# A graph-network kernel on one core: h0 remade by ScalarE and beta added by VectorE after the loop, the last chunk's pieces two maps later

## The chip, the cores and the metric

One core of a Trainium2 chip runs the whole kernel. The metric is the device time of one execution in microseconds; the trace is that of one profiled execution, and its times are microseconds from the start of its span. TensorE is PE in the rows (its weight loads PEld), VectorE is DVE, ScalarE is ACT, GpSimd is POOL, and SyncE, which issues most transfers, is SP. L893 is line 893 of the kernel.

## What is computed

Two graph layers over N = 1250 nodes with D = 512 features and E = 40000 edges (src, dst, and an edge tensor of 40000 x 512). Cut to what matters here:

```
h0  = relu(layernorm(x))
agg = segment_sum((h0[src] + edge) @ Wm.T + bm, dst) / max(deg, 1)
u   = concat(h0, agg) @ Wu.T + bu
o   = h0 + gelu(u)
x1  = x + layernorm(o) * gamma + beta
h1  = relu(layernorm(x1))
out = x1 + h1 + relu(((1 + eps) * h1 + segment_sum(h1[src], dst)) @ W1 + b1) @ W2 + b2
```

## The kernel before

Nodes lie in NT = 10 blocks of 128 rows. The kernel builds a matrix A16 of edge counts (node by node), so that a segment sum of gathered rows is a product with it. Node features that are multiplied with the counts are kept as a high and a low part, Hh and Hl, whose sum is the feature; Hl shares its memory with X.

**Stage 1, the edge loop** (to about 273 us). TensorE sums the edge tensor by destination and counts edges, VectorE and GpSimd add the results into aggT and A16, and in its last part the products "counts by h0" start, called pieces. A piece is one block of h0 against one chunk of columns: `PIECES` lists chunk 0 (512 columns), chunk 1 (512) and chunk 2 (256), ten pieces each. Also in this loop ScalarE makes h0 from x with scale rs and bias nb of the first layer norm (L478).

**Stage 2, the rounds after the loop** (about 276 to 351 us), where the change is. Each engine has its own queue, written out by hand, and each waits on semaphores. For each block b:

- TensorE: map b (`map_agg`, L1183: aggT times CT, four 128x512 fp32 products), which waits until VectorE has done update b-2. Between the first maps stand the ten pieces of chunk 2 (`late`, in the counts 1, 2, 3, 3, 1 behind maps 0 to 4). From map 5 on, map b is followed by T b-5 (`transpose_h1`), and from map 6 on by A b-6 (`times_A`: counts by h1, 512 columns, banks 0, 1, 4 and 5). After map 9 and A 3 come T 5, A 4, B 0, T 6, A 5, B 1, T 7, A 6, B 2, B 3, T 8 and so on (B is `times_A` with 256 columns), and behind them chunks C and E.
- VectorE works in rounds k = 0 to 14. The list STEPS (L919) says which step of which block stands in a round: update k (L866), center k-2 (L887), add_h0 k-1 (L871), add_x k-2 (L893), o_moments k-1 (L875), shift k-3 (L909), x1_moments k-2 (L897), four short steps, low_h1 k-4 (L914). Ahead of round 4 VectorE waits for all pieces and adds the sums of chunk 2 to aggT (L924, shown as L862), and TensorE waits for that sum after map 5, before T 0.
- ScalarE in step k: full_conv k+2 (L544, counts to fp32), gelu k (L548), h1 k-3 (L554), h1_high k-3 (L558), h1T k-3 (L563), which waits for T k-3.
- GpSimd: two small powers for each block (L424 rs, L428 rs2), and, for each block, `ahead(b)`: xt += beta (L413), and h0t = Hh + Hl (L416). Blocks 0 to 2 are done before the rounds; from block 3 on, `ahead(b)` falls into VectorE's round b.
- SP: loads the tile xt of x for block b once add_x b-3 has freed one of the three buffers (L339).

So add_h0 b needs gelu b and h0t b; add_x b needs rs b and xt b with beta in it; h1 b is written over Hh b, so it waits until h0t b has been made and until chunk 2's piece b has been read.

**Stage 3** (from about 351 us): TensorE finishes the products with the counts, then the two dense layers W1 and W2.

Of the kernel before, what the change touches and what calls it, by code (L numbers as in the profile page):

```python
# [5 lines left out]
F32 = mybir.dt.float32  # L6
# [4 lines left out]
ALU = mybir.AluOpType  # L11
ACT = mybir.ActivationFunctionType
AX = mybir.AxisListType

P = 128
# [12 lines left out]
def gnn_kernel(nc, x, src, dst, edge, Wm, bm, Wu, bu, gamma, beta, W1, b1, W2, b2, eps, out):  # L28
# [3 lines left out]
    NT = -(-N // P)  # L32
# [47 lines left out]
    def place(name, shape, dt, offset=None):  # L80
        size = mybir.dt.size(dt)
        for n in shape[1:]:
            size *= n
        if offset is None:
            offset = at[0]
            at[0] += -(-size // 32) * 32
        return nc.alloc_sbuf_tensor_at(name, shape, dt, offset=offset), offset

    X, x_at = place("X", [P, NT, D], F32)
    Hl, _ = place("Hl", [P, NT, D], F32R, x_at)  # L90
    Hh, _ = place("Hh", [P, NT, D], F32R)
    U, u_at = place("U", [P, NT, D], F32)
# [3 lines left out]
    CT, _ = place("CT", [P, FC, D], F32)  # L96
    W1s, _ = place("W1s", [P, FC, HID], F32, w1_at)
    W2s, _ = place("W2s", [P, KC, D], F32, a16_at)
    WuN, _ = place("WuN", [P, FC, 2 * D], F32, agg_at)
    Wu2T, _ = place("Wu2T", [P, FC, D], F32, u_at + 10240)  # L100
    WmN, _ = place("WmN", [P, FC, D], F32, u_at)
    bmB, _ = place("bmB", [P, FC, P], F32, u_at + 8192)
    acc, _ = place("acc", [P, NP], U16, w1_at)
    Dsum, _ = place("Dsum", [P, NP], F32, w1_at + NP * 2)
    TB = 3
    xt = [place(f"xt{i}", [P, D], F32, w1_at + i * 2048)[0] for i in range(TB)]
# [10 lines left out]
    ARd, _ = place("ARd", [P, NT, 256], F32R, arc_at + NT * 256 * 4)  # L117
    AR, _ = place("AR", [P, NT, NP], F32R, stream_at)
    hid, _ = place("hid", [P, KC, NP], F32, stream_at)
# [4 lines left out]
    dst_i, _ = place("dst_i", [P, GE], I32, arc_at + 8 * GE * 4)  # L124
    src_i, _ = place("src_i", [P, GE], I32, arc_at + 9 * GE * 4)
    genE, _ = place("genE", [P, SUB, D], F32, arc_at)
    genD, _ = place("genD", [P, SUB, P], F32, arc_at + SUB * D * 4)
    genS, _ = place("genS", [P, SUB, P], BF16, arc_at + SUB * D * 4 + SUB * P * 4)
    genK, _ = place("genK", [P, SUB, P], BF16, arc_at + SUB * D * 4 + SUB * P * 6)
# [5 lines left out]
    rest, _ = place("rest", [P, D], F32, idx_at)  # L135
    assert TB * 2048 <= 5 * SUB * GP * 4
    h0t = [place(f"h0t{i}", [P, D], F32)[0] for i in range(TB)]
    iotaF, _ = place("iotaF", [P, P], F32)
    iotaP, _ = place("iotaP", [P, 256, 2], BF16)
# [21 lines left out]
    nunc, _ = place("nunc", [1, 2], I32)  # L161
    stats, _ = place("stats", [P, NT, 6], F32)
    mv, _ = place("mv", [P, NT, 2], F32)
    stats2, _ = place("stats2", [P, NT, 6], F32)
    mv2, _ = place("mv2", [P, NT, 2], F32)
    ve, _ = place("ve", [P, NT], F32)
    ve2, _ = place("ve2", [P, NT], F32)
    rs, _ = place("rs", [P, NT], F32)
    rs2, _ = place("rs2", [P, NT], F32)
    nb, _ = place("nb", [P, NT], F32)  # L170
    degs, _ = place("degs", [P, NT], F32)
    rdeg, _ = place("rdeg", [P, NT], F32)
# [4 lines left out]
    with ctx:  # L177
# [61 lines left out]
        o_sum = sem("o_sum")  # L239
# [117 lines left out]
        def _(pool):  # L357
# [20 lines left out]
            nc.gpsimd.tensor_scalar(big[G, :], big[G, :], 1.0, None, ALU.subtract).then_inc(outside_ready, 1)  # L378
            pool.wait_ge(consts, 4)
            pool.wait_ge(ve_ready, 1)  # L380
            nc.gpsimd.tensor_tensor(rs[:], ve[:], mhalf[:], ALU.pow).then_inc(rs_ready, 1)

            def low_h0(b):
                pool.wait_ge(hi0_ready, b + 1)
# [23 lines left out]
                        low_h0(b)  # L408
            pool.wait_ge(low0_ready, NT)

            def ahead(b):
                pool.wait_ge(xt_in[b % TB], 16 * (b // TB + 1))
                nc.gpsimd.tensor_tensor(xt[b % TB][:], xt[b % TB][:], betaB[:], ALU.add).then_inc(xb_ready, 1)  # L413
                if b >= TB:
                    pool.wait_ge(o_sum, b - TB + 1)
                nc.gpsimd.tensor_tensor(h0t[b % TB][:], Hh[:, b, :].bitcast(F32), Hl[:, b, :].bitcast(F32), ALU.add).then_inc(h0t_ready, 1)  # L416

            pool.wait_ge(late_in, 48)
            for b in range(TB):
                ahead(b)  # L420
            for k in range(NT + 1):
                if k < NT:
                    pool.wait_ge(ve1_ready, k + 1)
                    nc.gpsimd.tensor_tensor(rs[:, k:k + 1], ve[:, k:k + 1], mhalf[:, 0:1], ALU.pow).then_inc(rs1_ready, 1)  # L424
                if k > 0:
                    b = k - 1
                    pool.wait_ge(ve2_ready, b + 1)
                    nc.gpsimd.tensor_tensor(rs2[:, b:b + 1], ve2[:, b:b + 1], mhalf[:, 0:1], ALU.pow).then_inc(rs2_ready, 1)  # L428
                    if b + TB < NT:
                        ahead(b + TB)  # L430

            pool.wait_ge(h1_ready, NT)
            pool.wait_ge(split1, NT)
# [10 lines left out]
        def _(act):  # L444
# [30 lines left out]
            def h0(b):  # L475
                if b == 0:
                    act.wait_ge(nb_ready, 1)
                nc.scalar.activation(X[:, b, :], X[:, b, :], ACT.Relu, bias=nb[:, b:b + 1], scale=rs[:, b:b + 1]).then_inc(h0_ready, 1)  # L478

            def transposed_h0(b):  # L480
                act.wait_ge(hT_mm, b + 1)
# [61 lines left out]
            def full_conv(c):  # L543
                nc.scalar.copy(AR[:, c, :], A16[:, c, 0:NP]).then_inc(conv, 1)  # L544

            def gelu(b):
                act.wait_ge(t_ready, b + 1)
                nc.scalar.activation(tt[b % TB][:], tt[b % TB][:], ACT.Gelu).then_inc(g_ready, 1)  # L548

            def h1(b):  # L550
                act.wait_ge(nb2_ready, b + 1)
                act.wait_ge(h0t_ready, b + 1)
                act.wait_ge(piece_mm, 2 * NT + b + 1)
                nc.scalar.activation(X[:, b, :], U[:, b, :], ACT.Relu, bias=nb[:, b:b + 1], scale=rs2[:, b:b + 1]).then_inc(h1_ready, 1)  # L554

# [9 lines left out]

            act.wait_ge(eps_ready, 2)
            full_conv(0)
            full_conv(1)
            for k in range(NT + 4):
                if k + 2 < NT:  # L570
                    full_conv(k + 2)
                for work, lag in ((gelu, 0), (h1, 3), (h1_high, 3), (h1T, 3)):
                    if 0 <= k - lag < NT:
                        work(k - lag)

            act.wait_ge(rst_mm, 4)

# [12 lines left out]
        def _(dve):  # L590
# [153 lines left out]
            for n in range(NG):  # L744
# [23 lines left out]

                if n == 2:
                    dve.wait_ge(rs_ready, 1)  # L770
                    V.scalar_tensor_tensor(nb[:], mv[:, :, 0], -1.0, rs[:], ALU.mult, ALU.mult).then_inc(nb_ready, 1)
                if n - 1 in ASIDE:
                    kind, k = ASIDE[n - 1]
                    if kind == "product" and k == FC:
# [110 lines left out]
            def center(b):  # L885
                dve.wait_ge(o_aggr, b + 1)
                V.scalar_tensor_tensor(tt[b % TB][:], tt[b % TB][:], mv[:, b, 0:1], gammaB[:], ALU.subtract, ALU.mult).then_inc(centered, 1)  # L887

            def add_x(b):
                dve.wait_ge(centered, b + 1)  # L890
                dve.wait_ge(rs1_ready, b + 1)
                dve.wait_ge(xb_ready, b + 1)
                V.scalar_tensor_tensor(U[:, b, :], tt[b % TB][:], rs[:, b:b + 1], xt[b % TB][:], ALU.mult, ALU.add).then_inc(x1_ready, 1)  # L893

            def x1_moments(b):
                dve.wait_ge(x1_ready, b + 1)
                V.bn_stats(stats2[:, b, :], U[:, b, :]).then_inc(x1_stats, 1)  # L897

            def x1_moments2(b):
                dve.wait_ge(x1_stats, b + 1)  # L900
                V.bn_aggr(mv2[:, b, :], stats2[:, b, :]).then_inc(x1_aggr, 1)

            def x1_variance(b):
                dve.wait_ge(x1_aggr, b + 1)
# [6 lines left out]
            def low_h1(b):  # L911
# [4 lines left out]
            dve.wait_ge(late_in, 48)  # L916
            dve.wait_ge(deg_step, 3 + NT)

            STEPS = [(update, 0), (center, 2), (add_h0, 1), (add_x, 2), (o_moments, 1), (shift, 3), (x1_moments, 2), (o_moments2, 1),  # L919
                     (x1_moments2, 2), (o_variance, 1), (x1_variance, 2), (low_h1, 4)]  # L920
            for k in range(NT + 5):
                if k == 4:
                    dve.wait_ge(piece_mm, 3 * NT)
                    add_sums(packed(0), QS[2][0]).then_inc(agg_done, 1)  # L924
                for work, lag in STEPS:
                    if 0 <= k - lag < NT:
                        work(k - lag)
# [23 lines left out]
        def _(pe):  # L951
# [223 lines left out]
            def transpose_h1(b):  # L1175
                pe.wait_ge(h1_ready, b + 1)
                if b >= 2:
                    pe.wait_ge(h1T_done, b - 1)
                for f in range(FC):
                    last = T.transpose(ps[:, 6 + b % 2, f * P:(f + 1) * P], X[:, b, f * P:(f + 1) * P], ident[:])  # L1180
                last.then_inc(h1T_mm, 1)
# [17 lines left out]
            def late(count):  # L1199
                for _ in range(count):  # L1200
                    piece(late_pieces.pop(0))

            for b in range(5):
                map_agg(b)
                late((1, 2, 3, 3, 1)[b])
            assert not late_pieces
            for b in range(5, NT):
                map_agg(b)
                if b == 5:
                    pe.wait_ge(agg_done, 2 * FC + 1)  # L1210
                transpose_h1(b - 5)
                if b > 5:
                    times_A(b - 6, "A")
            pe.wait_ge(t_ready, NT)
# [73 lines left out]
```

## Time and profile before

| | us |
|---|---|
| median of 3 runs | 529.69 (528.18 to 530.55) |
| profiled execution, its own time | 526.39 |
| its span in the trace | 524.6 |
| TensorE busy in the span | 482.8 (92%) |
| VectorE busy | 283.0 (54%) |
| GpSimd busy | 166.8 (32%) |
| ScalarE busy | 147.5 (28%) |
| mean granted TensorE clock, as a share | 0.992 |

The profiled execution took 1.8 us more than its span, and 3.3 us less than the median of the runs. Busy shares are averages over three stages with different limits, so the rows below are read for the rounds after the loop alone.

### The profile page before, as it was taken

How to read it: one execution, taken by the hardware profiler on the slowest of the kernel's cores; microseconds unless marked ns; L12 is line 12 of the kernel's file. 1: busy time of each engine (PE TensorE's matmuls, PEld its weight loads, DVE VectorE, ACT ScalarE, POOL GpSimd, SP SyncE). 2: the span in 40 equal slices, each digit the busy share in tenths (PEclk: the TensorE clock that was granted, in tenths of full speed). 3: DMA queues.
4: the chain of work that ended last, by engine and by line, in shares of the span. 5: the costliest groups of instructions: out<-in, count | busy, mean ns of one | idle time of the engine just before them, and what ended most of it. 6: DMA issues, size and time to landing. Idle time of an engine off the chain costs nothing.

```text
span 524.6 us, 8826 instructions
## 1 busy us (share of the span) xinstructions
PE 482.8 (92%) x3003; PEld 277.0 (53%) x3003; DVE 283.0 (54%) x660; ACT 147.5 (28%) x291; POOL 166.8 (32%) x217
## 2 busy tenths in 40 slices
PE   5889999898898988999999999599989999999997
PEld 4446554444444544675665655379944446744442
DVE  6897887888777779645434789983000000011111
ACT  4416644123222223222237245441011122100000
POOL 7323665333322224000023267636994000000000
PEclk9999999999999999999999999799999999999999
DMA  8998998889999999988820111112040000011111
GB/s 299 316 367 301 338 327 292 348 342 361 352 367 358 374 363 390 408 308 315 271 82 2 32 29 41 35 62 100 1 163 0 0 0 1 0 41 40 41 40 35
DMA packets 31115, 98.95 MB, mean 189 GB/s; under 512 B 3577, under 2 KB 3577, under 8 KB 31067
## 3 DMA queue, kind: packets, MB, share of 16 engines
q1 hardware_dynamic: 30458, 97.27, 50.7%
q10 hardware_dynamic: 608, 1.05, 0.7%
q8 instruction: 28, 0.46, 0.4%
q14 instruction: 21, 0.16, 0.1%
HBM read 95.76 MB, written 2.56 MB: 187 GB/s over the span
## 4 chain that ended last, share of the span: by engine, by line
PE 63%; DVE 21%; issue 6%; PEld 6%; DVEq 1%; POOL 1%; DMA 1%; SPq 0%; PEldq 0%; POOLq 0%
PE ps L1260 13%; PE ps L1245 13%; PE ps L1007 9%; PE ps L1048 7%; DVE A L669 5%; PE ps L1105 5%; PE ps L1106 4%; PE ps L1018 4%; PE ps L1194 3%; PEld ps L1171 3%; PE ps L1036 3%; PEld ps L1172 2%; DVE U L893 2%; DVE tt L871 2%; DVE oneS L648 2%
## 5 line engine op out<-in xcount | busy, mean ns | idle before, releaser
L400 POOL TENSOR_TENSOR aggT<-turned_sums,aggT 128x88 f32 x118 | 53.9, 456 | 107.4 <-ACT turned_sums L473 94.4
L1007 PE MATMUL ps<-ea,oneD 128*22 128x256 f32 x1264 | 83.9, 383 | 1.4 <-DVE oneD L640 0.9
L947 DVE TENSOR_TENSOR U<-ps,U 128x512 f32<-128x512 f32 (+1 forms) x10 | 6.9, 692 | 130.8 <-PE ps L1260 130.8
L467 ACT COPY packed_sums<-ps 128x256 f32<-128x256 f32 x79 | 29.4, 372 | 163.9 <-PE ps L1007 163.9
L1245 PE MATMUL ps<-aggT,W1s 128*128 (+1 forms) x192 | 67.4, 513 | 2.2 <-PEq L1239 2.2
L1260 PE MATMUL ps<-W2s,hid 128*128 128x512 f32 (+1 forms) x160 | 68.8, 592 | 0.0
L669 DVE TENSOR_TENSOR A<-ps,A 128x220 f32 x158 | 60.3, 381 | 8.6 <-PE ps L1018 8.0
L1018 PE MATMUL ps<-oneK,oneS 128*128 128x220 bf16 x316 | 42.5, 259 | 14.7 <-DVE oneS L648 13.0
L1245 PEld LDWEIGHTS ps<-aggT,W1s 128*128 128x128 f32 x192 | 36.4, 190 | 33.1 <-issue 33.0
L1007 PEld LDWEIGHTS ps<-ea,oneD 128*22 128x22 f32 x1264 | 30.5, 101 | 41.1 <-issue 23.6
L648 DVE TENSOR_TENSOR oneK<-iotaP,P_key 128x880 bf16<-128x880 bf16 x79 | 51.8, 655 | 0.0
L1260 PEld LDWEIGHTS ps<-W2s,hid 128*128 128x128 f32 (+1 forms) x160 | 30.0, 188 | 38.2 <-issue 38.2
L1171 PE MATMUL ps<-AR,Hh 128*128 128x256 f32 (+1 forms) x160 | 45.2, 318 | 0.5
L1172 PE MATMUL ps<-AR,Hl 128*128 128x256 f32 (+1 forms) x160 | 44.0, 312 | 0.0
L640 DVE TENSOR_TENSOR oneD<-iotaF,T_srel 128x88 f32<-128x88 f32 x79 | 22.4, 283 | 37.0 <-PE ps L1007 35.8
L1018 PEld LDWEIGHTS ps<-oneK,oneS 128*128 128x128 bf16 x316 | 28.9, 97 | 21.2 <-DVE oneK L648 11.7
L648 DVE TENSOR_TENSOR oneS<-iotaP,P_lo 128x512 bf16<-128x512 bf16 x79 | 39.2, 496 | 0.0
L1194 PE MATMUL ps<-CT,aggT 128*128 128x512 f32 x80 | 36.0, 593 | 1.2 <-DVE aggT L720 1.2
L581 ACT ACTIVATE hid<-ps,b1C 128x512 f32 (+1 forms) x24 | 14.6, 608 | 80.3 <-PE ps L1245 80.3
L1048 PE MATMUL ps<-Wu1T,U 128*128 128x512 f32 x80 | 36.1, 593 | 0.0
L1036 PE MATMUL ps<-ident,packed_sums 128*128 128x128 f32 x158 | 34.5, 300 | 0.0
L1105 PE MATMUL ps<-ARc,Hh 128*128 128x512 f32 x80 | 33.4, 417 | 1.0 <-DVE aggT L720 1.0
(139 smaller groups left out, 645.1 us busy)
## 6 DMA issues: line engine op xcount, KB each, us to landing
ea<-in_edge_attr_dram SPq DMA_DIRECT2D x78, 1024.0 KB, 7.6
X<-in_x_dram SPq DMA_DIRECT2D x1, 2304.0 KB
xt<-in_x_dram SPq DMA_DIRECT2D x9, 256.0 KB, 2.7
out_dram<-U SPq DMA_DIRECT2D x9, 256.0 KB
W1s<-in_L_gnn_W_dram SPq DMA_DIRECT2D x1, 2048.0 KB, 7.7
W2s<-in_L_gnn_W_dram SPq DMA_DIRECT2D x1, 2048.0 KB, 8.7
WuN<-in_L_gnn_Wu_dram ACTq DMA_DIRECT2D x1, 1024.0 KB, 5.4
WuN<-in_L_gnn_Wu_dram SPq DMA_DIRECT2D x1, 1024.0 KB, 6.8
```

Source lines behind the costliest of these rows:

```text
L400: nc.gpsimd.tensor_tensor(cols, sums, cols, ALU.add).then_inc(early_step, 1)
L648: V.tensor_tensor(hot[m % HOTS][:], iota, mine, ALU.is_equal).then_inc(ready, 1)
L669: V.tensor_tensor(cols, ps[:, 4 + m % 2, half * KW:(half + 1) * KW].rearrange("p (h w) -> p h w", w=W), cols, ALU.add).then_inc(add_step, 1)
L1007: last = T.matmul(to.rearrange("p (c d) -> p c d", c=2), oneD[h][:, g * 2 + j, :], data, start=j == 0, stop=j == 1)
L1018: last = T.matmul(ps[:, 4 + m % 2, (j // 2) * KW:(j // 2 + 1) * KW], oneS[h][:, j // 2, :, j % 2], oneK[h][:, j // 2, :, j % 2], start=j % ...
L1048: last = T.matmul(ps[:, ASIDE_BANK["u1", b], :], U[:, b, f * P:(f + 1) * P], Wu1T[:, f, :], start=f == 0, stop=f == FC - 1)
L1105: T.matmul(to, Hh[:, c, rows], counted, start=c == 0 and (q < 2 or f % 2 == 0), stop=False)
L1171: T.matmul(to, Hh[:, b, rows], AR[:, b, start:start + cols], start=b == 0 and (cols == 512 or f % 2 == 0), stop=False)
L1172: last = T.matmul(to, Hl[:, b, rows], AR[:, b, start:start + cols], start=False, stop=b == NT - 1 and (cols == 512 or f % 2 == 1))
L1194: last = T.matmul(ps[:, 2 + b % 2, :], aggT[:, f, b * P:(b + 1) * P], CT[:, f, :], start=f == 0, stop=f == FC - 1)
L1245: last = T.matmul(ps[:, CHUNK_BANK[k % 4], 0:cols], W1s[:, f, k * P:(k + 1) * P], aggT[:, f, bass.ds(start, cols)], start=f == 0, stop=f = ...
L1260: last = T.matmul(ps[0:rows, 6 + b % 2, :], hid[:, k, b * P:b * P + rows], W2s[:, k, :], start=k == 0, stop=k == KC - 1)
```

## The change

The first layer norm's scale and bias get tiles of their own, rs0 and nb0, so that they outlive the loop (rs and nb are written again for the second and third norm). After the loop ScalarE makes h0t b from the loaded tile xt b with `relu(rs0 * x + nb0)`, one step ahead of its use, between gelu and h1. VectorE adds beta to xt b in a new step `add_beta` (lag 1) between x1_moments and o_moments2, once h0t b is made. GpSimd's `ahead` is gone, so GpSimd only makes the powers. The pieces of chunk 2 stand in the counts 0, 0, 2, 3, 3 and 2 behind maps 0 to 5; VectorE adds their sums ahead of round 6 instead of round 4, and TensorE waits for that after map 6 and T 1, before A 0. The moments of x1 share the tile stats with those of o.

```diff
@@ gpsimd
-            nc.gpsimd.tensor_tensor(rs[:], ve[:], mhalf[:], ALU.pow).then_inc(rs_ready, 1)
+            nc.gpsimd.tensor_tensor(rs0[:], ve[:], mhalf[:], ALU.pow).then_inc(rs_ready, 1)
...
-            def ahead(b):
-                pool.wait_ge(xt_in[b % TB], 16 * (b // TB + 1))
-                nc.gpsimd.tensor_tensor(xt[b % TB][:], xt[b % TB][:], betaB[:], ALU.add).then_inc(xb_ready, 1)
-                if b >= TB:
-                    pool.wait_ge(o_sum, b - TB + 1)
-                nc.gpsimd.tensor_tensor(h0t[b % TB][:], Hh[:, b, :].bitcast(F32), Hl[:, b, :].bitcast(F32), ALU.add).then_inc(h0t_ready, 1)
-
-            pool.wait_ge(late_in, 48)
-            for b in range(TB):
-                ahead(b)
...
-                    if b + TB < NT:
-                        ahead(b + TB)
@@ scalar
-                nc.scalar.activation(X[:, b, :], X[:, b, :], ACT.Relu, bias=nb[:, b:b + 1], scale=rs[:, b:b + 1]).then_inc(h0_ready, 1)
+                nc.scalar.activation(X[:, b, :], X[:, b, :], ACT.Relu, bias=nb0[:, b:b + 1], scale=rs0[:, b:b + 1]).then_inc(h0_ready, 1)
...
+            def h0_again(b):
+                act.wait_ge(xt_in[b % TB], 16 * (b // TB + 1))
+                if b >= TB:
+                    act.wait_ge(o_sum, b - TB + 1)
+                nc.scalar.activation(h0t[b % TB][:], xt[b % TB][:], ACT.Relu, bias=nb0[:, b:b + 1], scale=rs0[:, b:b + 1]).then_inc(h0t_ready, 1)
...
             def h1(b):
                 act.wait_ge(nb2_ready, b + 1)
-                act.wait_ge(h0t_ready, b + 1)
...
             full_conv(0)
+            h0_again(0)
             full_conv(1)
...
                         work(k - lag)
+                    if work is gelu and k + 1 < NT:
+                        h0_again(k + 1)
@@ vector
-                    V.scalar_tensor_tensor(nb[:], mv[:, :, 0], -1.0, rs[:], ALU.mult, ALU.mult).then_inc(nb_ready, 1)
+                    V.scalar_tensor_tensor(nb0[:], mv[:, :, 0], -1.0, rs0[:], ALU.mult, ALU.mult).then_inc(nb_ready, 1)
...
+            def add_beta(b):
+                dve.wait_ge(h0t_ready, b + 1)
+                V.tensor_tensor(xt[b % TB][:], xt[b % TB][:], betaB[:], ALU.add).then_inc(xb_ready, 1)
...
-                V.bn_stats(stats2[:, b, :], U[:, b, :]).then_inc(x1_stats, 1)
+                V.bn_stats(stats[:, b, :], U[:, b, :]).then_inc(x1_stats, 1)
...
-            STEPS = [(update, 0), (center, 2), (add_h0, 1), (add_x, 2), (o_moments, 1), (shift, 3), (x1_moments, 2), (o_moments2, 1),
+            STEPS = [(update, 0), (center, 2), (add_h0, 1), (add_x, 2), (o_moments, 1), (shift, 3), (x1_moments, 2), (add_beta, 1), (o_moments2, 1),
                      (x1_moments2, 2), (o_variance, 1), (x1_variance, 2), (low_h1, 4)]
             for k in range(NT + 5):
-                if k == 4:
+                if k == 6:
                     dve.wait_ge(piece_mm, 3 * NT)
                     add_sums(packed(0), QS[2][0]).then_inc(agg_done, 1)
@@ tensor
             for b in range(5):
                 map_agg(b)
-                late((1, 2, 3, 3, 1)[b])
-            assert not late_pieces
+                late((0, 0, 2, 3, 3)[b])
             for b in range(5, NT):
                 map_agg(b)
                 if b == 5:
+                    late(2)
+                    assert not late_pieces
+                transpose_h1(b - 5)
+                if b == 6:
                     pe.wait_ge(agg_done, 2 * FC + 1)
-                transpose_h1(b - 5)
                 if b > 5:
                     times_A(b - 6, "A")
```

## Rows read from the trace of the kernel before

**Rows 1.** Busy time of each engine in two stretches, granted clock, DMA.

```profile
309.50:351.30 41.80, 34.06 (x132) 22.15 (x132) 41.70 (x79) 22.14 (x32) 27.00 (x24) 0.92 0.08 25
351.30:385.00 33.70, 31.59 (x253) 30.30 (x252) 8.12 (x10) 3.16 (x5) 25.31 (x21) 1.00 0.16 63
```

**Rows 2.** Timeline of DVE, round 6: start, us, line, operation.

```profile
316.51 0.74 DVE L866 SCALAR_TENSOR_TENSOR tt<-ps,rdeg,U 128x512 f32<-128x512 f32 x1
317.17 0.74 DVE L887 SCALAR_TENSOR_TENSOR tt<-tt,mv,gammaB 128x512 f32<-128x512 f32 x1
317.83 1.79 DVE L871 TENSOR_TENSOR tt<-tt,h0t 128x512 f32<-128x512 f32 x1
319.54 1.75 DVE L893 SCALAR_TENSOR_TENSOR U<-tt,rs,xt 128x512 f32<-128x512 f32 x1
```

**Rows 3.** Timeline of POOL in the same round.

```profile
316.97 0.54 POOL L428 TENSOR_TENSOR rs<-ve,mhalf 128x1 f32<-128x1 f32 x1
317.49 1.58 POOL L413 TENSOR_TENSOR xt<-xt,betaB 128x512 f32<-128x512 f32 x1
319.03 1.71 POOL L416 TENSOR_TENSOR h0t<-Hh,Hl 128x512 f32<-128x512 f32 x1
```

**Rows 4.** Timeline of DVE, round 10.

```profile
344.43 0.74 DVE L887 SCALAR_TENSOR_TENSOR tt<-tt,mv,gammaB 128x512 f32<-128x512 f32 x1
345.09 0.68 DVE L871 TENSOR_TENSOR tt<-tt,h0t 128x512 f32<-128x512 f32 x1
345.69 0.75 DVE L893 SCALAR_TENSOR_TENSOR U<-tt,rs,xt 128x512 f32<-128x512 f32 x1
```

**Rows 5.** Timeline of PE: T 5, T 6, T 7, first product of A 6.

```profile
338.25 1.12 PE L1180 MATMUL ps<-ident,X 128*128 128x128 f32 x4 [5.49 <-DVE tt L866]
...
343.79 0.66 PE L1180 MATMUL ps<-ident,X 128*128 128x128 f32 x4
...
348.01 0.66 PE L1180 MATMUL ps<-ident,X 128*128 128x128 f32 x4 [0.38 <-ACT X L554]
348.79 0.50 PE L1171 MATMUL ps<-AR,Hh 128*128 128x512 f32 x1
```

**Rows 6.** Stretches of 2 us, columns as in rows 1: PE's clock.

```profile
335.00:337.00 2.00, 0.00 (x0) 0.00 (x0) 2.00 (x9) 1.03 (x2) 0.14 (x1) 0.68 0.23 75
...
341.00:343.00 2.00, 2.00 (x9) 1.62 (x8) 2.00 (x4) 0.08 (x1) 0.67 (x1) 0.61 0.00 0
...
383.00:385.00 2.00, 0.00 (x0) 0.00 (x0) 1.15 (x1) 0.00 (x0) 1.84 (x3) 1.00 0.00 0
```

**Rows 7.** Timeline of DVE: chunk 2's sum and the start of round 5.

```profile
303.51 1.23 DVE L862 TENSOR_TENSOR aggT<-ps,aggT 128x1024 f32<-128x1024 f32 x1 [1.97 <-PE ps L1106]
...
309.52 0.74 DVE L866 SCALAR_TENSOR_TENSOR tt<-ps,rdeg,U 128x512 f32<-128x512 f32 x1
```

**Rows 8.** Timeline of PE: T 0, T 1, map 7, T 2.

```profile
306.74 0.60 PE L1180 MATMUL ps<-ident,X 128*128 128x128 f32 x4
...
310.61 0.60 PE L1180 MATMUL ps<-ident,X 128*128 128x128 f32 x4
...
312.92 3.59 PE L1194 MATMUL ps<-CT,aggT 128*128 128x512 f32 x8
316.35 0.60 PE L1180 MATMUL ps<-ident,X 128*128 128x128 f32 x4
```

**Rows 9.** L478 by source: ns min/median/max, first and last start.

```profile
L478 ACT ACTIVATE X<-X,nb,rs x10: 814/824/830, 43.6 to 68.1; 128x512 f32<-128x512 f32 x10
```

**Rows 10.** Timeline of ACT in round 6.

```profile
316.99 0.69 ACT L563 ACTIVATE aggT<-ps,eps 128x512 f32<-128x512 f32 x1 [0.52 <-PE ps L1180]
317.58 1.25 ACT L544 CAST AR<-A 128x1280 fp32r<-128x1280 uint16 x1
318.73 0.63 ACT L548 ACTIVATE tt<-tt 128x512 f32<-128x512 f32 x1
```

**Rows 11.** The ten loads of xt, from issue to landing.

```profile
DMA to landing us min/median/max: 2.6/2.7/5.1
```

More of the change, by code:

```diff
@@ L163, in gnn_kernel @@
     mv, _ = place("mv", [P, NT, 2], F32)
-    stats2, _ = place("stats2", [P, NT, 6], F32)
     mv2, _ = place("mv2", [P, NT, 2], F32)
@@ L169, in gnn_kernel @@
     rs2, _ = place("rs2", [P, NT], F32)
+    rs0, _ = place("rs0", [P, NT], F32)
+    nb0, _ = place("nb0", [P, NT], F32)
     nb, _ = place("nb", [P, NT], F32)
@@ L896, in x1_moments @@
                 dve.wait_ge(x1_ready, b + 1)
-                V.bn_stats(stats2[:, b, :], U[:, b, :]).then_inc(x1_stats, 1)
+                V.bn_stats(stats[:, b, :], U[:, b, :]).then_inc(x1_stats, 1)
             def x1_moments2(b):
                 dve.wait_ge(x1_stats, b + 1)
-                V.bn_aggr(mv2[:, b, :], stats2[:, b, :]).then_inc(x1_aggr, 1)
+                V.bn_aggr(mv2[:, b, :], stats[:, b, :]).then_inc(x1_aggr, 1)
             def x1_variance(b):
```

## The prediction, made before the changed kernel was run

> **What bounds the kernel now.** I read the share of each engine in the stretch of the rounds first. From 309.5 to 351.3 us VectorE is busy for 41.70 of 41.80 us and TensorE for 34.06; from 351.3 to 385 it is the other way round, TensorE 31.59 of 33.70 and VectorE 8.12 [rows 1]. So VectorE sets the pace up to about 349 us, TensorE behind it, and what is saved in VectorE's rounds counts until TensorE is the bound.
>
> Then I read one round on VectorE beside GpSimd's queue. Round 6 begins at 316.51; the five rounds 5 to 9 begin at 309.52 [rows 7] and are over at 344.43 [rows 4], 6.98 us each. In it add_h0 takes 1.79 us and add_x 1.75 [rows 2], while in round 10 the same two take 0.68 and 0.75 [rows 4]. The difference between them is GpSimd: in round 6 its add of beta runs from 317.49 to 319.07 and its Hh + Hl from 319.03 to 320.74 [rows 3]; add_h0 begins at 317.83 and lets add_x begin at 319.54, half a microsecond (its own length) after the first of them ended, and add_x in turn is as long as it takes to outlast the second. In round 10 GpSimd has no such work. So VectorE stands still while GpSimd's add runs. The records differ by 1.79 - 0.68 = 1.1 and 1.75 - 0.75 = 1.0: 2.1 us in each of five rounds are spent waiting for GpSimd, and a clean round is 6.98 - 2.10 = 4.88. (A record is some 0.08 longer than the step to the next start, 0.68 against 0.60; from here on I count steps: add_h0 0.60, add_x 0.67, update and center 0.66.)
>
> Last I read TensorE. It waits 5.49 us ahead of T 5 for update 9, and a slower clock follows: T 5 takes 1.12 us where T 6 takes 0.66 [rows 5]; the granted clock is 0.68 at 335 to 337 and 0.61 at 341 to 343 (1.00 is 2.4 GHz, 0.50 is 1.2), and full at 383 to 385, where TensorE was idle too [rows 6]. A 6 starts at 348.79 [rows 5], and from there TensorE runs without a gap. **A 6's start is the point that I forecast; what it gains, the end gains.**
>
> **The change, part by part.**
>
> *Names of loop tiles, stats.* rs0, nb0 and the shared stats move no work: the same instructions in the same order. Nothing, from both sides.
>
> *GpSimd's twenty adds go.* Of these ten stand in rounds 5 to 9 and cost VectorE 5 x 2.1 = **-10.5 us**. The other ten stand ahead of the rounds and in rounds 3 and 4, where VectorE waits for the pieces in the end (1.97 us idle ahead of the sum [rows 7]); they save nothing.
>
> *VectorE's add_beta.* It has the form of add_h0, 0.60 us from start to next start [rows 4]. Before A 6 six rounds carry it (5 to 10): 6 x 0.60 = **+3.6 us**. It could collide with GpSimd's powers. Row first: the power at 316.97 runs to 317.51 beside center, issued at 317.17, and center takes its usual 0.74 [rows 2, 3]. The Trainium skill's page "SBUF — State Buffer", section "Who interferes with whom", says that a VectorE instruction with two SBUF inputs and a GpSimd one that reads SBUF lock each other out for the whole instruction. By that, center would have waited 0.34 us, and the sum would carry up to 5 x 0.34 = 1.7 us more; the row says zero for a 128x1 power, and the trace agrees with the page only for the large adds. I take zero, and keep 1.7 for the range.
>
> *ScalarE's h0.* An activation of this form took 824 ns [rows 9]. ScalarE is busy for 22 of 41.8 us [rows 1], so seven more (blocks 3 to 9 in the rounds) fit in total; the question is who stands behind. Behind h0 b+1 in its queue stand h1 b-3, h1_high, h1T, full_conv and gelu b+1, and T b-3 and add_h0 b+1 wait for these. h0 b also waits for its tile, freed by add_x b-3 in VectorE's round b-1, 2.6 us into it (update 0.66, center 0.66, add_h0 0.60, add_x 0.67), and landed after 0.3 us of issue and 2.7 us (5.1 at most) [rows 11]. From there h0, h1, h1_high, h1T, full_conv and gelu need 0.83 + 0.83 + 0.65 + 0.59 + 1.15 + 0.55 = 4.6 us (h1 taken like h0, h1_high like a gelu with its wait) [rows 9, 10], and add_h0 b wants gelu b 1.3 us into round b+1. Rounds of 5.5: 5.5 - 2.6 + 5.5 + 1.3 = 9.7, less 4.6 leaves 5.1 us for the landing. It is hidden at 2.7 and just hidden at 5.1.
>
> *The pieces and the sum of chunk 2.* A piece costs TensorE the same wherever it stands; T 0 comes after six maps and all ten pieces in both, so it stays at 306.74 [rows 8]. VectorE's rounds 0 to 4 have slack up to there. The sum (303.51 to the next start at 304.65, 1.14 us) [rows 7] moves from ahead of round 4, where VectorE was waiting anyway, to ahead of round 6, where it is on the path: **+1.1 us**. And TensorE, which did not wait for it before, now has only A 0 left to do after T 1 and waits until VectorE has finished round 5 and the sum.
>
> *The walk.* I go through the queues with these durations: map 3.43, T and A together 2.31, T alone 0.4 (0.78 where TensorE had stopped, as at T 7), A 1.9, B half of that; 0.64 from T's start until ScalarE's h1T starts [rows 5, 8, 10].
>
> 1. T 0 at 306.7 releases low_h1 0 (0.61), the last step of round 4; update 5 at 308.0, against 309.52 [rows 7]: **-1.5 us**.
> 2. ScalarE: h1T 0 from 307.4, full_conv, gelu 4 done 309.7; add_h0 4 would like 309.3, waits 0.4. From there a round needs 4.16 (4.88 + 0.60 - 1.32). Round 5 ends 313.9, the sum 315.05.
> 3. T 1 waits for h1 1 behind h0 5: 311.4. TensorE then idles about 2.9 us until the sum at 315.05. A 0, map 7, T 2 at 320.4. Low_h1 2 waits for T 2, 1.2 us; update 7 at 321.7.
> 4. T 2, h1T 2, full_conv, gelu 6 (0.64 + 0.59 + 1.15 + 0.55): add_h0 6 at 323.4, 0.4 late; update 8 at 327.6. In the same way, 0.3 late, update 9 at 333.4.
> 5. T 5 waits for h1 5 behind h0 9 on ScalarE: 335.4, against 338.25, and at full clock. T 6 339.1. Round 9 ends 338.9, round 10 (no update) takes 4.82: low_h1 6 done 343.7, **A 6 at 343.8**.
>
> As a sum, up to the end of round 10: -10.5 + 3.6 + 1.1 - 1.5 + waits of 0.4 + 1.2 + 0.4 + 0.3 = 2.3, together **-5.0 us**. A 6 at 343.8 against 348.79 is the same 5.0. Behind it, T 8, T 9 and their h1 come as early, and stage 3 stands on TensorE alone. Span 524.6 - 5.0 = 519.6, own time 526.4 - 5.0 = 521.4. The profiled execution is 3.3 us under the median of the runs, so the median to expect is 529.69 - 5.0 = **524.7**. Half a per cent, about what a measurement can tell from no change here, is 2.65 us.
>
> The gain has a ceiling. Without any wait or slow clock in this stretch TensorE would save its idle 41.80 - 34.06 = 7.7 us [rows 1], and for the slow clock 1.9 (5.54 from T 5 to T 6, where T, A and B with the restart need 3.6 [rows 5]): 9.6 us.
>
> **Rivals.**
>
> *The clock falls at the new gap.* TensorE idles some 2.9 us ahead of A 0. In the trace it idled from 338.25 - 5.49 = 332.8 [rows 5], and the clock was down between 335 and 337 [rows 6], so a gap of about 3 us can be enough; the shorter one up to 385 was not. Price: the half clock cost 1.9 us from T 5 to T 6; A 0 and map 7 stand on the path that sets update 7 and all after it, so about 1.8 comes through. A 6 at 345.6, gain 3.2: **526.5**. The Trainium skill's page "TensorE: Matmul & The Clock Gate", Part 1, has throttling as the default state, which comes back when the array goes idle; it speaks against putting a wait where none was.
>
> *More is gained.* If gelu and h1 come earlier than I have them (rounds 7 to 10 without the 0.7 of waits, and TensorE's gap shorter because T 1 starts early), 7 us: **522.7**.
>
> *Within half a per cent.* Powers that lock (1.7) together with the slow clock (1.8) leave 1.5: **528.2**.
>
> *Slower: the load of the tile becomes the ring.* ScalarE's queue now stops at h0 for the tile, where GpSimd's did before and nobody stood behind. Up to 5.1 us of landing it is hidden; each microsecond more is then paid by one load after the other. Walking the queues with a landing of 8 us puts A 6 at 349, no gain; with 9 us at 352.2, 3.4 us later than before: **533.1**. For it: a wait in front of five others' work. Against: the loads took 2.6 to 5.1 [rows 11], with DMA nearly idle (0.08) [rows 1].
>
> *The change doesn't do it.* If the 1.1 us were not GpSimd's doing, VectorE would keep 6.98 and add 0.6: slower by 3. Against it stand the clean rows of round 10 [rows 4]; part of the slower chance.
>
> **How the numbers follow.** Forecast 0.48, clock 0.20, more 0.13, within half a per cent 0.11, slower 0.08. Forecast, more and most of the clock case are faster by over 2.65 us: 0.76. The same side takes 0.11 and the worse end of the clock case, 0.16; slower 0.08. The range reaches from 8 us gained (a step past the "more" case, within the ceiling of 9.6) to 0.9 gained (clock and powers together): 521.7 to 528.8. The likeliest case alone: 523.2 to 526.
>
> **What the new trace would show.** Right: add_h0 and add_x at 0.7 in all rounds; rounds of 5.5 to 6; sum of chunk 2 at about 314 and a gap of about 3 us on TensorE ahead of A 0; T 5 near 335.4 at full clock; A 6 near 343.8. Wrong: any 1.7 us step on VectorE; h0 waiting for the tile with VectorE waiting for gelu behind it; a granted clock under 1 between 312 and 320; T 0 later than 306.7, which would mean that the earlier rounds had no slack for ScalarE's new work.

## The result, and the profile after

| | before | changed |
|---|---|---|
| median of 10 runs, us | 528.18 (526.88 to 530.55) | 524.40 (521.50 to 526.09) |
| profiled execution, own time | 526.39 | 523.95 |
| its span | 524.6 | 522.2 |
| GpSimd busy in the span | 166.8 | 136.7 |

The ratio is 0.993, with a 95% interval from 0.991 to 0.995: 3.8 us faster, where 5.0 was forecast for the likeliest case and 3.2 for the case in which the clock falls. The time lies in the stated range of 521.7 to 528.8. That it lies within 0.3 us of the forecast median of 524.7 is luck: that median was counted down from 529.69, the median of three runs, and the ten runs of the kernel before have 528.18, from which 5.0 would have given 523.2.

The two stretches of [rows 1], in the changed kernel:

```profile
309.50:351.30 41.80, 36.19 (x153) 24.24 (x152) 36.59 (x87) 26.97 (x39) 9.94 (x13) 0.96 0.13 38
351.30:385.00 33.70, 31.66 (x241) 29.27 (x240) 7.08 (x7) 2.38 (x4) 26.50 (x21) 1.00 0.16 54
```

VectorE, which had no gap before (41.70 of 41.80 us busy), now has 5 us of them. Its timeline from the sum of chunk 2 to the start of round 7 answers to [rows 2] and [rows 7] (start, us, line, operation, idle time before and who ended it):

```profile
315.06 1.22 DVE L859 TENSOR_TENSOR aggT<-ps,aggT 128x1024 f32<-128x1024 f32 x1
316.19 0.74 DVE L863 SCALAR_TENSOR_TENSOR tt<-ps,rdeg,U 128x512 f32<-128x512 f32 x1
...
317.51 0.69 DVE L868 TENSOR_TENSOR tt<-tt,h0t 128x512 f32<-128x512 f32 x1
318.12 0.74 DVE L894 SCALAR_TENSOR_TENSOR U<-tt,rs,xt 128x512 f32<-128x512 f32 x1
...
320.04 0.68 DVE L888 TENSOR_TENSOR xt<-xt,betaB 128x512 f32<-128x512 f32 x1
320.63 0.18 DVE L876 BATCH_NORM_AGGREGATE mv<-stats 128x2 f32<-128x6 f32 x1
...
324.05 0.69 DVE L915 TENSOR_TENSOR Hl<-X,Hh 128x512 fp32r<-128x512 f32 x1 [2.99 <-PE ps L1181]
324.66 0.75 DVE L863 SCALAR_TENSOR_TENSOR tt<-ps,rdeg,U 128x512 f32<-128x512 f32 x1
326.38 0.69 DVE L868 TENSOR_TENSOR tt<-tt,h0t 128x512 f32<-128x512 f32 x1 [0.31 <-ACT tt L543]
```

add_h0 (L868) and add_x (L894) take 0.69 and 0.74 where they took 1.79 and 1.75. The new add of beta (L888) costs 0.59 to the next start. But low_h1 2 (L915) stands 2.99 us for T 2. The reason is in TensorE's timeline (T 0, A 0, T 2, T 5, T 7, A 6), which answers to [rows 5] and [rows 8]:

```profile
307.94 0.60 PE L1181 MATMUL ps<-ident,X 128*128 128x128 f32 x4
...
316.33 0.50 PE L1172 MATMUL ps<-AR,Hh 128*128 128x512 f32 x1 [3.28 <-DVE aggT L859]
...
323.35 0.60 PE L1181 MATMUL ps<-ident,X 128*128 128x128 f32 x4
...
338.17 0.63 PE L1181 MATMUL ps<-ident,X 128*128 128x128 f32 x4 [0.88 <-issue]
...
345.19 0.66 PE L1181 MATMUL ps<-ident,X 128*128 128x128 f32 x4 [0.37 <-ACT X L548]
346.50 0.50 PE L1172 MATMUL ps<-AR,Hh 128*128 128x512 f32 x1 [0.65 <-DVE Hl L915]
```

TensorE waits 3.28 us for the sum ahead of A 0, and then the clock is down (0.57 from 317 to 321, where 0.50 is 1.2 GHz). Stretches of 2 us (columns as in [rows 1]; the last is the gap ahead of the first dense layer, at full clock):

```profile
315.00:317.00 2.00, 0.67 (x3) 0.58 (x4) 2.00 (x4) 1.97 (x4) 1.07 (x2) 1.00 0.02 4
317.00:319.00 2.00, 2.00 (x7) 1.59 (x6) 2.00 (x4) 0.52 (x1) 0.00 (x0) 0.57 0.00 0
319.00:321.00 2.00, 2.00 (x4) 0.89 (x4) 2.00 (x8) 0.00 (x0) 0.00 (x0) 0.57 0.49 119
381.00:383.00 2.00, 0.36 (x1) 0.30 (x2) 0.86 (x1) 0.00 (x0) 1.84 (x3) 1.00 0.03 8
```

Since T 0 does not begin at the same moment in all traces (the time up to the first map, which the change leaves alone, was 1.2 us longer in this execution than in the one of before, and T 0 comes 30.1 us after the first map in every trace: 307.94 against 306.74), I measure from T 0 to A 6 from here on. Before it is 348.79 - 306.74 = **42.05 us**, now 346.50 - 307.94 = **38.56**: 3.5 us gained. The forecast was 37.1. Behind A 6 there is no difference: 175.8 us to the end of the span before, 175.7 now.

### The profile page after: what moved, and what is told of

It reads as the page before. It is cut to its first block, busy times and chain, and to the rows that moved or that the text cites. A ratio compares the mean times of both kernels' runs of the same rounds, so it can differ in the third digit from the quotient of the medians.

```text
span 522.2 us, 8832 instructions
## 1 busy us (share of the span) xinstructions
PE 482.2 (92%) x3003; PEld 276.5 (53%) x3003; DVE 277.4 (53%) x670; ACT 153.6 (29%) x301; POOL 136.7 (26%) x197
## 4 chain that ended last, share of the span: by engine, by line
PE 70%; DVE 14%; issue 6%; PEld 6%; DVEq 1%; DMA 1%; ACT 1%; POOL 0%; SPq 0%; PEldq 0%; ACTq 0%; POOLq 0%
PE ps L1263 13%; PE ps L1248 13%; PE ps L1008 10%; PE ps L1049 7%; PE ps L1195 5%; PE ps L1106 5%; DVE A L666 5%; PE ps L1107 4%; PE ps L1019 4%; PE ps L1037 3%; PEld ps L1172 3%; PE ps L975 3%; PEld ps L1173 2%; DVE oneS L645 1%; DVE oneD L637 1%
## 5 line engine op out<-in xcount | busy, mean ns | idle before, releaser
L415 POOL TENSOR_TENSOR rs<-ve,mhalf 128x1 f32<-128x1 f32 x10 | 7.8, 781 | 124.0 <-DVE ve L880 124.0
```

## The experiments

| kernel | median, us | ratio to before (95%) | T 0 to A 6, us | A 6 to the end, us |
|---|---|---|---|---|
| before | 528.18 | | 42.05 | 175.8 |
| changed, first | 524.40 | 0.993 (0.991 to 0.995) | 38.56 | 175.7 |
| changed, again | 523.93 | 0.993 (0.990 to 0.996) | 38.53 | 175.4 |
| engines only | 520.98 | 0.986 (0.982 to 0.989) | 35.23 | 177.3 |
| pieces only | 525.95 | 0.996 (0.994 to 0.998) | 40.75 | 177.3 |
| sum in round 4 | **518.78** | 0.983 (0.980 to 0.986) | 33.85 | 176.0 |
| GpSimd's adds as idle work | 532.08 | 1.009 (1.006 to 1.012) | 45.03 | 175.5 |
| memsets as idle work | 525.46 | 0.996 (0.993 to 0.998) | 38.50 | 178.3 |
| gap filled | 524.55 | 0.993 (0.990 to 0.996) | 36.97 | 178.2 |
| beta on GpSimd | 523.97 | 0.992 (0.989 to 0.995) | 38.44 | 175.7 |
| x tiles one load later | 528.10 | 1.000 (0.998 to 1.002) | 40.63 | 177.3 |
| x tiles two loads later | 528.56 | 1.002 (0.999 to 1.004) | 41.94 | 175.7 |

The last two columns come from one profiled execution of each kernel. The kernel before was run beside each group of kernels again (medians 528.15 to 528.68), and a ratio is to the runs beside it. The single runs of one kernel spread over some 4 to 5 us; the path from T 0 to A 6 is finer: the changed kernel gave 38.56 and 38.53.

**The changed kernel again**, as the mark for those below.

> The changed kernel itself, so that the others of this call are compared with it on the same chip. Both theories: about 3.8 us under the kernel before (0.993). In the trace, counted from T 0's start: TensorE waits about 3.3 us ahead of A 0, A 6 starts 38.6 us after T 0 where the clock falls in that gap and about 37 where it does not.

Both as before; the gap ahead of A 0 is 3.28 us again, and the clock falls in it again.

**Engines only.** The two halves of the change are parted: here the work moves from GpSimd to ScalarE and VectorE, and the pieces stay.

```diff
-                late((0, 0, 2, 3, 3)[b])
+                late((1, 2, 3, 3, 1)[b])
...
-                if k == 6:
+                if k == 4:
```

> ScalarE makes h0 and VectorE adds beta, but the pieces stand behind maps 0 to 4 as before, the sum of chunk 2 ahead of round 4, TensorE's wait for it ahead of T 0. Theory (all the gain is from GpSimd's adds that no longer stop VectorE, and moving the pieces costs some of it again through the gap ahead of A 0): no gap over 1.5 us on TensorE before T 5, full clock, A 6 some 35.8 us after T 0; 5.5 to 6.5 us under the kernel before, 1.5 to 3 under the changed one. Rival (the pieces had to move for the gain, since ScalarE's new work makes h1 0 late for the old order): 524 or more, no faster than the changed kernel, with TensorE waiting for h1.

Measured 7.2 us under before, somewhat more than expected, and 3.0 under the changed kernel. TensorE's longest wait between T 0 and A 6 is the one ahead of T 5, and the clock is full in all this stretch:

```profile
333.94 0.63 PE L1181 MATMUL ps<-ident,X 128*128 128x128 f32 x4 [1.82 <-DVE tt L863]
...
342.79 0.50 PE L1172 MATMUL ps<-AR,Hh 128*128 128x512 f32 x1 [0.65 <-DVE Hl L915]
```

T 1 does wait 0.8 us for h1 1, as the rival had it, but that is all. The whole gain is in this half, and the other half, the pieces and the sum of chunk 2 moved together, takes 3.3 us of it back on the path.

**Pieces only.** The other half alone, in the kernel before.

```diff
-                late((1, 2, 3, 3, 1)[b])
+                late((0, 0, 2, 3, 3)[b])
...
-                if k == 4:
+                if k == 6:
```

> The kernel before with only the pieces, the sum and TensorE's wait moved as in the change; GpSimd still adds beta and makes h0. Theory: VectorE's rounds 6 to 9 stay near 7 us, add_h0 and add_x at 1.7 us; round 5 begins some 1 us earlier, but the sum of 1.1 us and the gap ahead of A 0 are new: between 2 us faster and 2 us slower than before. Rival (the moved pieces bring the gain): 3 us or more faster than before.

2.2 us faster than before, 1.3 on the path: the same edit gains a little where GpSimd has its adds and costs 3.3 where it has not. Round 7, on VectorE and then on GpSimd:

```profile
324.06 0.84 DVE L914 TENSOR_TENSOR Hl<-X,Hh 128x512 fp32r<-128x512 f32 x1 [2.16 <-PE ps L1180]
324.83 0.74 DVE L866 SCALAR_TENSOR_TENSOR tt<-ps,rdeg,U 128x512 f32<-128x512 f32 x1
325.49 1.12 DVE L887 SCALAR_TENSOR_TENSOR tt<-tt,mv,gammaB 128x512 f32<-128x512 f32 x1
326.53 0.68 DVE L871 TENSOR_TENSOR tt<-tt,h0t 128x512 f32<-128x512 f32 x1
327.13 0.74 DVE L893 SCALAR_TENSOR_TENSOR U<-tt,rs,xt 128x512 f32<-128x512 f32 x1
```

```profile
323.08 1.28 POOL L413 TENSOR_TENSOR xt<-xt,betaB 128x512 f32<-128x512 f32 x1 [0.17 <-DMA xt<-in_x_dram]
324.32 1.74 POOL L416 TENSOR_TENSOR h0t<-Hh,Hl 128x512 f32<-128x512 f32 x1
```

The new wait of VectorE for T lies where GpSimd adds beta (from 323.08), so that this add stops VectorE for at most the 0.15 us by which low_h1 is longer; the second add stretches center, from 0.74 to 1.12, and add_h0 and add_x are back at 0.68 and 0.74 in this round. This does not hold for every round: in rounds 5 to 9 the stretched records of VectorE add up to some 6.3 us more than they take alone, against 10.5 in the kernel before. A wait and a lock that would each cost a microsecond or two cover each other in part. In the changed kernel there is no lock left to cover, and the wait is paid.

**Sum in round 4.** One step of the changed kernel moved: the sum of chunk 2 goes where VectorE stands anyway.

```diff
-                if k == 6:
-                    dve.wait_ge(piece_mm, 3 * NT)
-                    add_sums(packed(0), QS[2][0]).then_inc(agg_done, 1)
                 for work, lag in STEPS:
+                    if k == 4 and work is low_h1:
+                        dve.wait_ge(piece_mm, 3 * NT)
+                        add_sums(packed(0), QS[2][0]).then_inc(agg_done, 1)
```

> The changed kernel with one step moved: VectorE adds chunk 2's sum in round 4, right ahead of low_h1 0, where it stood still for 3.8 us waiting for T 0, instead of ahead of round 6. Theory (the gap ahead of A 0 and the fall of the clock in it are what the change gives back): the gap goes, the clock stays full, A 6 about 34.3 us after T 0, 4 us earlier than in the changed kernel's trace; 2.5 to 4.5 us under the changed kernel, 6.5 to 8.5 under the kernel before. Rival (the gap is hidden, since VectorE is the bound anyway): within 1 us of the changed kernel.

The fastest kernel of all: 5.2 us under the changed one and 9.4 under before, 0.7 and 0.9 more than the expected ranges reach; A 6 comes 33.85 us after T 0, 4.7 earlier than in the changed kernel. On VectorE, the sum fills what was idle time ahead of low_h1 0:

```profile
306.69 1.22 DVE L859 TENSOR_TENSOR aggT<-ps,aggT 128x1024 f32<-128x1024 f32 x1 [3.27 <-PE ps L1107]
307.83 0.68 DVE L915 TENSOR_TENSOR Hl<-X,Hh 128x512 fp32r<-128x512 f32 x1
```

The gap ahead of A 0 is gone and the clock is full at 309 to 315. This kernel has the pieces where the change put them, and A 6 comes 1.4 us earlier than with engines only (33.85 against 35.23). So it is not the moved pieces that cost the 3.3 us, but the place of the sum behind them.

**GpSimd's adds as idle work.** Does VectorE wait for what GpSimd computes, or for GpSimd being at work? The changed kernel, with two adds in each of the old places; their output is read by nobody.

```diff
+                    if b + TB < NT:
+                        for i in range(2):
+                            nc.gpsimd.tensor_tensor(idle[:], gammaB[:], betaB[:], ALU.add).then_inc(idle_step, 1)
+                            pool.wait_ge(idle_step, 2 * b + i + 1)
```

> The changed kernel, to which GpSimd's two 128x512 adds for each of the blocks 3 to 9 are given back as idle work: it adds two tiles that nobody changes into one that nobody reads, in the places where it added beta and made h0 before. Nothing waits for them. Theory (VectorE stands still while such an add runs): add_h0, add_x or their neighbours take about 1.1 us more in pairs again, rounds 5 to 9 grow by up to 2.1 us each, less where they waited for TensorE or ScalarE; A 6 comes 6 to 10 us later after T 0 than 38.5, and the kernel is 6 to 10 us slower than the changed one, slower than the kernel before. Rival (GpSimd's adds cost because VectorE had to wait for their results): no change, within 1 us of the changed kernel.

8.2 us slower than the changed kernel (532.08 against 523.93, on another chip; 1.009 and 0.993 of the kernel before, each beside its own runs), 6.5 on the path. Round 6, VectorE and then GpSimd:

```profile
317.78 1.01 DVE L890 SCALAR_TENSOR_TENSOR tt<-tt,mv,gammaB 128x512 f32<-128x512 f32 x1
318.71 1.76 DVE L874 TENSOR_TENSOR tt<-tt,h0t 128x512 f32<-128x512 f32 x1
320.39 0.74 DVE L900 SCALAR_TENSOR_TENSOR U<-tt,rs,xt 128x512 f32<-128x512 f32 x1
```

```profile
316.96 2.96 POOL L424 TENSOR_TENSOR idle<-gammaB,betaB 128x512 f32<-128x512 f32 x2
```

GpSimd's pair runs from 316.96 to 319.92, the first add until 318.24; center is stretched past the first and add_h0 past the second, and add_x behind them is not. Nobody used the result: it is the engine's work, not its data, that stops VectorE.

**Memsets as idle work.** The same with `nc.gpsimd.memset(idle[:], 0.0)` in place of the add.

> The same idle work as a 128x512 memset instead of an add, so GpSimd writes the tile but reads nothing. The Trainium skill, page SBUF - State Buffer, section Who interferes with whom, has VectorE's instructions with two SBUF inputs contend with a GpSimd instruction that reads SBUF, and not with one that only writes. By that, VectorE's records stay as in the changed kernel and the time is within 1 us of it. If any large GpSimd instruction stops VectorE, it is as slow as with the adds, in proportion to the length of the memsets.

On the path nothing: 38.50. The median is 1.5 us over the changed kernel's, more than the 1 us expected, though the two intervals overlap. The execution traced lost its time behind A 6 (178.3 against 175.7), where GpSimd makes no memset: TensorE waited 3.06 us ahead of the first dense layer instead of 2.04, and the clock fell there. Whether that explains the median is open. Two memsets (0.52 us each) beside center and add_h0, GpSimd and then VectorE:

```profile
331.47 1.10 POOL L424 MEMSET idle<- 128x512 f32 x2
```

```profile
331.17 0.74 DVE L890 SCALAR_TENSOR_TENSOR tt<-tt,mv,gammaB 128x512 f32<-128x512 f32 x1
332.16 0.69 DVE L874 TENSOR_TENSOR tt<-tt,h0t 128x512 f32<-128x512 f32 x1 [0.25 <-ACT tt L549]
```

Center runs into the first memset, and add_h0 is issued while the second runs; both take what they take alone. The Trainium skill's "SBUF — State Buffer", "Who interferes with whom", says that a VectorE instruction with two SBUF inputs meets only those of GpSimd's that read SBUF; by that rule, adds stop it and memsets don't, and both traces agree.

**Gap filled.** What does the clock's fall cost by itself? Idle products on TensorE in the gap, into a bank that T 2 overwrites.

```diff
                 if b == 6:
+                    pe.wait_ge(h1T_done, 1)
+                    for _ in range(3):
+                        T.matmul(ps[:, 6, :], ident[:], CT[:, 0, :], start=True, stop=True)
                     pe.wait_ge(agg_done, 2 * FC + 1)
```

> The changed kernel with three idle products of 512 columns (fp32, some 0.86 us each) on TensorE between T 1 and its wait for the sum of chunk 2, into a bank that the next transposes overwrite. The gap of 3.3 us shrinks to under 1. Theory (the clock's fall in the gap costs about 1.7 us, the gap itself stays): granted clock full from 312 to 321, A 6 about 36.9 us after T 0 instead of 38.5, and 1 to 2 us under the changed kernel. Rival (the slow clock is hidden behind VectorE, which is the bound): A 6 at 38.5 as before.

A 0 then waits only another 0.70 us, the clock stays full, and A 6 comes 36.97 us after T 0, 1.6 us earlier than in the changed kernel:

```profile
317.00:319.00 2.00, 2.00 (x9) 1.65 (x10) 2.00 (x4) 1.11 (x2) 0.00 (x0) 1.00 0.01 4
319.00:321.00 2.00, 2.00 (x6) 0.88 (x5) 2.00 (x5) 0.00 (x0) 0.00 (x0) 1.00 0.14 35
381.00:383.00 2.00, 0.39 (x1) 0.39 (x2) 0.00 (x0) 0.00 (x0) 1.69 (x2) 0.86 0.37 32
383.00:385.00 2.00, 2.00 (x3) 0.78 (x3) 0.00 (x0) 0.00 (x0) 1.99 (x2) 0.50 0.76 210
```

The median of 524.55 shows none of it. In the traced execution it was given back: the clock fell instead in the gap ahead of the first dense layer (the last two lines), and A 6 to the end took 178.2 us where the changed kernel took 175.7. Some 1.0 of these 2.5 us is not the clock but a longer wait ahead of the layer (3.00 us against 2.04), whose cause no run shows. Whether the medians agree for these reasons in all runs is open; only the path shows the 1.6.

**Beta on GpSimd.** ScalarE makes h0, GpSimd adds beta behind it, VectorE has no add_beta (the lines that call `ahead` are left out here).

```diff
-            STEPS = [(update, 0), (center, 2), (add_h0, 1), (add_x, 2), (o_moments, 1), (shift, 3), (x1_moments, 2), (add_beta, 1), (o_moments2, 1),
+            STEPS = [(update, 0), (center, 2), (add_h0, 1), (add_x, 2), (o_moments, 1), (shift, 3), (x1_moments, 2), (o_moments2, 1),
...
+            def ahead(b):
+                pool.wait_ge(h0t_ready, b + 1)
+                nc.gpsimd.tensor_tensor(xt[b % TB][:], xt[b % TB][:], betaB[:], ALU.add).then_inc(xb_ready, 1)
```

> The changed kernel with beta still added by GpSimd, once ScalarE has made h0; VectorE has no add_beta. Theory: one add for each round stops VectorE for about 1.1 us where VectorE saves 0.6: 5 x 0.5 = 2.5 us in rounds 5 to 9 less what the waits hide, so 0 to 3 us slower than the changed kernel. Rival (VectorE's extra 0.6 a round is the dearer of the two): 1 to 3 us faster.

No difference (38.44 against 38.5), but not for the reason given. In rounds 5 to 9 only two of the five adds stretch VectorE (center to 1.26 us in round 6, add_h0 to 1.77 in round 9); the other three are stretched themselves (1.74 us instead of 1.28). So VectorE paid some 1.6 us and was spared five times 0.6, and still nothing was gained: it waits 2.94 us for T 2 as before. Where the rest of the spared time went is not shown.

**X tiles landing later.** The slower rival: idle loads of the same size ahead of each x tile from block 3 on; the second kernel has 2 in both places where this diff has 1.

```diff
                     sp.wait_ge(x1_ready, b - TB + 1)
+                    for i in range(1):
+                        sp.dma_start(idle[:], x[0:P, :]).then_inc(idle_in, 16)
+                        sp.wait_ge(idle_in, 16 * (1 * (b - TB) + i + 1))
```

> The changed kernel; ahead of each load of an x tile from block 3 on SP makes one more load of the same size into memory that nobody reads, and waits for it. A tile lands about 2.9 us later, some 5.8 us after its buffer is freed. By the prediction's walk a landing of up to about 5 us is hidden and at 5.8 A 6 comes about 1.4 us later (from T 0 about 40 with the clock's fall in the gap): 0 to 2.5 us slower than the changed kernel. If ScalarE's queue has much more room than I gave it: no change in A 6. If the load was already on the path: 3 us or more slower.

> The same with two more loads, a landing some 8.7 us after the buffer is freed. By the walk A 6 comes some 7 us later than in the changed kernel, now with VectorE waiting for gelu behind h0 on ScalarE in most rounds: 5 to 9 us slower than the changed kernel, slower than the kernel before. If there is much more room: under 3 us.

In the changed kernel h0 waits for its tile twice (4.0 and 2.7 us, blocks 3 and 4), where nobody behind it is late. With one more load A 6 comes 2.1 us later, with two 3.4. The medians are 4.2 and 4.6 us over the changed kernel's (on another chip): the first is above the expected 0 to 2.5, the second just below the expected 5 to 9, and on the path too the second is only half of what the walk gave.

Nor was it the walk's mechanism. VectorE did not wait longer for gelu (0.9 us in all, as without the loads). With one load its low_h1 6 is no later than in the changed kernel (37.92 us after T 0, against 37.81); what is late is T 5, by 2.0 us, behind h1 5 and h0 9 in ScalarE's queue, and after that gap TensorE's clock falls (T 5, and one stretch of 2 us):

```profile
339.48 0.84 PE L1186 MATMUL ps<-ident,X 128*128 128x128 f32 x4 [2.94 <-issue]
341.00:343.00 2.00, 2.00 (x6) 1.61 (x5) 2.00 (x5) 1.88 (x4) 0.52 (x1) 0.50 0.00 0
```

From T 5 to T 6 it takes 4.82 us where it took 3.26, so T 6 is 3.6 us late; 1.5 of them go where TensorE had waited anyway (ahead of T 7 and A 6), and 2.1 are left. With a full clock some 0.5 would be left: an estimate from these steps, since no run has the late tile without the fall. With two loads the same happens at T 4, with the clock at 0.50 from 337 to 339, and there VectorE too is held, 2.72 us for T 4. The waits of TensorE in the kernel with two loads, 275 to 350 us (total, times, longest):

```profile
PE ps L1186 <- ACT X L553: 3.7, 2, 2.3
```

## Why the prediction was right

The sign and the mechanism held, and the size to within 1.2 us at the medians; of its cases the profiled executions show the second, the clock's fall.

- *The bound and the lock*: right. add_h0 and add_x fell by 1.1 and 1.0 us, and the adds put back as idle work brought such stretches back (not in every round, since VectorE now waits in some).
- *add_beta 0.60, powers at zero*: right, 0.59, and center at 336.86 takes 0.74 beside a power that runs from 336.66 to 337.21. The extra 1.7 us by the Trainium skill's whole-instruction rule (on the page "SBUF — State Buffer" it stands in the section on SBUF's two sides) did not come. Why not is not shown; these powers read 128x1 elements.
- *The sum, +1.1 in round 6*: right, 316.19 - 315.06 = 1.13.
- *The walk*: shifted by the 1.2 us of T 0, it had the sum at 315.1 (measured 315.06), A 0 at 316.25 (316.33), T 2 at 321.6 (323.35), T 5 at 336.6 (338.17), A 6 at 345.0 (346.50). The sum and A 0 are met within 0.1, and after them everything is 1.5 to 1.75 late. That is the clock: with the gap filled, T 2 comes 13.80 us after T 0, and the walk has 13.66.
- *The likeliest case left out the clock's fall*: this is the step that was off, by 1.6 us (the gap-filled kernel reaches 36.97 where the walk says 37.1). The rival had priced it at 1.8 with a chance of 0.20; the trace of before had shown a fall after 3 us of idleness, and the walk had itself found a gap of 2.9. It should have been the likeliest.
- *T 0 to A 6 gained 5.0 in the forecast and 3.5 in the trace; the medians gained 3.8.* The span was forecast at 519.6 and is 522.2: 1.2 of the difference lies ahead of the first map, the rest is the clock.
- *Its signs of being wrong*: one came, a granted clock under 1 between 312 and 320. T 0 later than 306.7 came too, but not for the reason feared: it stands 30.1 us behind the first map as before, so the earlier rounds had slack for ScalarE's new work. There is no 1.7 us step on VectorE.
- *The pieces*: the prediction costed the sum and the gap but never asked what the same engines would do with the pieces and the sum left alone. That is the larger error of thought: this half of the change costs 3.3 us on the path, 1.6 through the clock, and the other 1.7, as far as the rows tell, through the sum and the wait for T 2. It is the place of the sum that costs: with the sum in round 4 the moved pieces gain 1.4 us.
- *Slack of the tile*: worked out for the wrong waiter. The 5.1 us were those of VectorE's add_h0, and VectorE was indeed not held with one load. But the walk itself has T 5 behind h0 9, and there the slack is about 0.6 us: with one load tile 9 is issued 2.57 us later and T 5 starts 2.0 later. Beyond that the walk was too steep (5 us of loss at 8 us of landing; 3.4 measured with two loads, part of it the clock). The forecast did not suffer, since no tile landed late in the changed kernel.

## What to carry to other kernels

When an engine has no idle time and yet single instructions of it take two and a half times what they take elsewhere in the trace, look at what its neighbour runs at that moment; adding 0.6 us of work to the busy engine can be cheap if it takes 1.1 us twice away from it. A step that was placed under an old wait has to be placed again when that wait goes: here a better place for the sum was the idle time that the change itself had opened ahead of low_h1 0, and it was worth more (5.2 us) than the change (3.8). Count a new gap on TensorE together with the clock that may follow it.

## What the runs showed of the hardware

- GpSimd's 128x512 add (1.3 us alone) stops VectorE's instructions with two operands in SBUF until it ends, and takes up to 1.78 us itself where such an instruction already runs; a GpSimd memset of the same tile (0.52 us) and its 128x1 powers do not. Instructions with one operand in PSUM keep their length beside such adds: in the kernel before, the sum of chunk 2 took 1.23 us at 303.51 and update 4 0.74 at 304.65, beside GpSimd's adds from 302.70 to 305.21.
- The fall of TensorE's clock in a short gap differs from execution to execution. In the gap ahead of the first dense layer it stayed full in seven traces (before, the changed kernel twice, sum in round 4, adds, beta on GpSimd, two loads) and fell in five. From the first product of that layer to the end it takes 139.5 to 139.6 us in the seven and 141.1 to 141.2 in the five, so this one fall costs about 1.6 us each time. TensorE's wait there was 1.84 to 2.36 us in the seven and in three of the five, and 3.06 and 3.00 in the other two (memsets, gap filled); this longer wait, of unknown cause, adds the other 1.0 us to their last column. I had not expected a fall there, since the trace of before shows none.
- Of the ten runs of the changed kernel the one with the highest mean clock (0.997) took 522.6 us and the one with the lowest (0.986) 525.4. So part of the spread between runs may be such falls of the clock; in the runs of the kernel before the order is less clear.
